# Last layer of a fused four-block kernel: a new order on four engines, rounding inside the scaling, the output shared between ScalarE and GpSimd

## The reference, cut to what matters

```python
def rmsnorm(x): return x * rsqrt(mean(x * x, -1) + EPS)
def act_quant(x):
    scale = 127.0 / clip(max(abs(x), -1), 1e-05)
    return clip(round(x * scale), -128.0, 127.0) / scale
def bitlinear(x, w, b): return act_quant(rmsnorm(x)) @ weight_quant(w).T + b
...
x = x + tanh(g_xattn[1]) * aligned(ctx_1024, layernorm(x))      # 0/1 matrix of the path times ctx
h = gelu(bitlinear(layernorm(x), w1, b1))                       # 256 -> 1024
x = x + tanh(g_ffn[1]) * bitlinear(h, w2, b2)                   # 1024 -> 256
```

## Time and profile before

| | |
|---|---|
| time, 3 runs | 1986.56 us median (1986.07 to 1990.5) |
| the profiled execution | 1983.74 us, its span 1981.8 us |
| start of the last layer | 1628.93 us into the span, so 352.9 us of it |
| busy over the whole span | PE 74%, DVE 73%, ACT 56%, POOL 31% |
| mean granted TensorE clock | 0.877 of full speed |

### The profile page before, as it was taken

One profiled execution on the slowest core, in us unless ns is written; L12 is line 12 of the kernel. 1 busy time (PEld: TensorE's weight loads), 2 busy tenths in 40 slices (PEclk: granted clock), 3 DMA queues, 4 the chain that ended last, 5 costly groups with the idle time before them and its releaser, 6 DMA issues. The chain is left out here.

```text
span 1981.8 us, 35784 instructions
## 1 busy us (share of the span) xinstructions
PE 1476.4 (74%) x10821; PEld 1063.2 (54%) x10821; DVE 1447.5 (73%) x4096; ACT 1101.0 (56%) x2310; POOL 623.9 (31%) x1067
## 2 busy tenths in 40 slices
PE   2689999999999999999999986132331007888886
PEld 1467777777777777777777765000000004555554
DVE  7466666676666667666666643799998988888885
ACT  0166666666666666666666662243333006777876
POOL 3112322222222222322222222200000007888886
PEclk9699999999999999999999998555555559999999
DMA  2444444444443444434444410322210012222210
GB/s 77 122 128 137 120 111 126 110 132 119 125 120 109 129 114 136 118 109 126 111 133 115 113 39 17 89 61 58 60 36 4 0 31 70 81 80 81 81 60 33
DMA packets 322937, 179.49 MB, mean 91 GB/s; under 512 B 93794, under 2 KB 318194, under 8 KB 322803
## 3 DMA queue, kind: packets, MB, share of 16 engines
q1 hardware_dynamic: 322802, 178.07, 32.4%
HBM read 122.91 MB, written 50.33 MB: 87 GB/s over the span
## 5 line engine op out<-in xcount | busy, mean ns | idle before, releaser
L795 DVE TENSOR_REDUCE nmax<-s 128x2 f32<-128x512 f32 x512 | 325.3, 682 | 40.8 <-PE s L376 39.4
L591 ACT ACTIVATE pt<-s 128x512 f32<-128x512 f32 x512 | 277.3, 597 | 84.5 <-PE s L391 84.5
L882 POOL TENSOR_TENSOR r<-rl 128x512 f32<-128x512 f32 x128 | 133.1, 1040 | 371.0 <-ACT rl L621 368.4
L376 PE MATMUL s<-kst,qst 96*128 96x256 bf16 x1024 | 164.1, 276 | 17.7 <-DVE nmax L795 12.7
L391 PE MATMUL s<-qst,kst 128*128 128x256 bf16 x1024 | 167.9, 276 | 9.1 <-ACT pt L591 1.4
L1294 PE MATMUL gate<-diag,one 128*128 128x512 f16 x35 | 21.2, 606 | 176.4 <-DVE left L1381 176.4
L621 ACT ACTIVATE rl<-wb,fscl 128x256 f32<-128x256 f32 x256 | 107.3, 472 | 81.2 <-PE wb L473 81.2
L469 PE MATMUL wb<-x2l,wfcT 128*128 128x256 f32 x512 | 143.2, 301 | 0.5 <-ACT dd L641 0.5
L403 PE MATMUL oacc<-pt,vw 128*32 128x256 f32 x2048 | 137.9, 387 | 2.0 <-ACT pt L591 2.0
L893 POOL TENSOR_TENSOR ln_y<-ln_v,ln_pow 128x6 f32<-128x6 f32 (+2 forms) x37 | 44.5, 1202 | 300.5 <-DVE ln_v L828 300.4
L340 PE MATMUL wb<-wprT,r2l 128*128 128x256 f32 x512 | 129.4, 292 | 6.9 <-DVE r2l L764 6.9
(11 more groups left out here) (265 smaller groups left out, 3998.0 us busy)
## 6 DMA issues: line engine op xcount, KB each, us to landing
kst<-k_parts_dram SPq DMA_DIRECT2D x384, 64.0 KB, 2.7
qst<-q_parts_dram SPq DMA_DIRECT2D x384, 64.0 KB, 2.4
k_parts_dram<-kp SPq DMA_DIRECT2D x32, 384.0 KB, 5.1
q_parts_dram<-qp SPq DMA_DIRECT2D x32, 384.0 KB, 3.1
xin<-in_x_dram SPq DMA_DIRECT2D x32, 256.0 KB, 2.9
cT<-in_ctx_T_dram SPq DMA_DIRECT2D x32, 256.0 KB, 2.7
xres<-in_x_dram SPq DMA_DIRECT2D x32, 256.0 KB, 3.1
cin<-in_ctx_dram SPq DMA_DIRECT2D x32, 256.0 KB, 4.5
```

What stands on the lines that cost most here:

```text
L376: last = pe.matmul(s1[h % 2][:, t, :], qst[b.p][0:MAXROW, h, t * P:t * P + P], kst[b.p][0:MAXROW, h, :], start=True, stop=True)
L591: act.activation(pt[h % (2 * HPG)][:], s2[h % 2][:], ACT.Exp).then_inc(e["expd"], 1)
L795: v.tensor_reduce(nmax[:, T * h:T * h + T], s1[h % 2][:], AX.X, ALU.max, negate=True)\
L882: pool.tensor_tensor(r2[:], rl[:, k % 2], rl[:, k % 2], ALU.mult)\
```

## The change

In the last layer only:

- The constant added by `scale_x` and `scale_h` grows by 26112, so that the low 16 bits of each fp32 word are, read as an f16 number, 1536 plus the rounded value. TensorE transposes these 16 bits of each word (`low16`, every second f16 element of the tile), and the ScalarE copies out of PSUM take 1536 away. `round_x` (ScalarE) and `round_h` (GpSimd) are gone. `xqT_copy` becomes two instructions, since the inverse parts (`xinv`) stay bf16.
- `factors` is divided: GpSimd's `bounds` ends with `back`; VectorE's `factors` has the reciprocal in place of the power of -1, and the product `q`. The hidden part of both belongs to batch k-1 instead of k.
- VectorE's `output` is divided: ScalarE `scale_output` writes po times scale to `yo`, GpSimd `output` adds `x3b`.
- The order on each engine is new; hidden activations are turned and multiplied two turns after their batch's number (k-2) instead of one, the output follows at k-3, and the loop has one turn more. `gl`, `hr`, `x3b` have more buffers. GpSimd's `bias` waits for the masks of a later batch (`masked`), which VectorE now makes in front of gelu's maxima.

```diff
+F16_ONE_AND_A_HALF = 1536.0
+MAGIC_F16 = MAGIC + float(0x6600)
...
-        x3b = [sb(f"x3b{p}", [P, T, D]) for p in range(6)]
+        x3b = [sb(f"x3b{p}", [P, T, D]) for p in range(8)]
...
-        gl = [[sb(f"gl{p}{t}", [P, F]) for t in range(T)] for p in range(2)]
+        gl = [[sb(f"gl{p}{t}", [P, F]) for t in range(T)] for p in range(3)]
-        hr_ = [sb(f"hr{t}", [P, F]) for t in range(T)]
-        hq = [[sb(f"hq{p}{t}", [P, F], BF16) for t in range(T)] for p in range(2)]
+        hr_ = [[sb(f"hr{p}{t}", [P, F]) for t in range(T)] for p in range(2)]
...
-        FIRST, LAST = -6, NB + 2
+        FIRST, LAST = -6, NB + 3
...
+        def low16(words):
+            return words.bitcast(F16).rearrange("p (f two) -> p f two", two=2)[:, :, 0]
...
-                if there(k - 2):
-                    store(k - 2)
+                if there(k - 3):
+                    store(k - 3)
...
             def turn_x(n):
-                w("x_round", n + 1), w("inv_parts", n + 1), w("xqT_cp", n)
-                for c in range(C + 1):
-                    for t in range(T):
-                        last = pe.transpose(pt_x[:, c, t * P:t * P + P], xq[:, t, c * P:c * P + P], identb[:])
+                w("x_scaled", n + 1), w("inv_parts", n + 1), w("xqT_cp", n)
+                for t in range(T):
+                    for c in range(C):
+                        pe.transpose(pt_x[:, c, t * P:t * P + P].bitcast(F16), low16(xr[:, t, c * P:c * P + P]), one16[:])
+                for t in range(T):
+                    last = pe.transpose(pt_x[:, C, t * P:t * P + P], xinv[:, t, :], identb[:])
                 last.then_inc(e["xq_t"], 1)
...
-            def hidden(n):
...
+            def hidden(n, t):
+                w("xqT_cp", n + 1), w("gelu", 2 * (n - 1) + t + 1)
...
             def turn_h(n, t):
-                w("h_round", 2 * n + t + 1), w("hqT_cp", 2 * n + t)
+                w("h_scaled", 2 * n + t + 1), w("hqT_cp", 2 * n + t)
                 for f in range(FT):
-                    last = pe.transpose(pt_h[:, f, :], hq[n % 2][t][:, f * P:f * P + P], identb[:])
+                    last = pe.transpose(pt_h[:, f, :], low16(hr_[n % 2][t][:, f * P:f * P + P]), one16[:])
                 last.then_inc(e["hq_t"], 1)
...
             def output(n):
-                w("x4_res", n)
+                w("o_scaled", n)
...
             for k in range(FIRST, LAST):
+                if there(k - 2):
+                    turn_h(k - 2, 0)
                 if there(k + 1):
-                    hidden(k + 1)
-                if there(k - 1):
-                    turn_h(k - 1, 0)
+                    turn_x(k + 1)
                 if there(k + 4):
                     expand(k + 4)
-                if there(k - 1):
-                    turn_h(k - 1, 1)
-                    output(k - 1)
-                if there(k + 2):
-                    turn_x(k + 2)
+                if there(k - 2):
+                    turn_h(k - 2, 1)
+                if there(k + 1):
+                    hidden(k + 1, 0)
+                    hidden(k + 1, 1)
+                if there(k - 2):
+                    output(k - 2)
...
-            def round_x(n):
-                w("x_scaled", n + 1), w("xq_t", n)
-                act.activation(xq[:, :, 0:D], xr[:], ACT.Copy, bias=-MAGIC).then_inc(e["x_round"], 1)
-
             def xqT_copy(n):
                 w("xq_t", n + 1), w("h_mm", 2 * n)
-                act.activation(xqT[:], pt_x[:], ACT.Copy).then_inc(e["xqT_cp"], 1)
+                act.activation(xqT[:, 0:C, :], pt_x[:, 0:C, :].bitcast(F16), ACT.Copy, bias=-F16_ONE_AND_A_HALF)
+                act.activation(xqT[:, C, :], pt_x[:, C, :], ACT.Copy).then_inc(e["xqT_cp"], 1)
 
             def hqT_copy(n, t):
                 w("hq_t", 2 * n + t + 1), w("o_mm", n)
-                act.activation(hqT[t][:], pt_h[:], ACT.Copy).then_inc(e["hqT_cp"], 1)
+                act.activation(hqT[t][:], pt_h[:], ACT.Copy, bias=-F16_ONE_AND_A_HALF).then_inc(e["hqT_cp"], 1)
+
+            def scale_output(n):
+                w("o_mm", n + 1), w("x4_res", n - 1)
+                for t in range(T):
+                    last = act.activation(yo[n % 2][:, t, :], po[:, t, :], ACT.Copy,
+                                          scale=back[(n + 1) % 4][:, T + t:T + t + 1])
+                last.then_inc(e["o_scaled"], 1)
 
             w("ends", 1)
             for k in range(FIRST, LAST):
+                if there(k - 3):
+                    scale_output(k - 3)
+                if there(k - 2):
+                    hqT_copy(k - 2, 0)
+                if there(k + 1):
+                    xqT_copy(k + 1)
                 if there(k):
+                    squares(k, 0)
                     squares(k, 1)
                 if there(k + 6):
                     distance(k + 6)
-                if there(k - 1):
-                    hqT_copy(k - 1, 0)
+                if there(k - 2):
+                    hqT_copy(k - 2, 1)
                 if there(k + 1):
                     gelu(k + 1, 0)
-                if there(k - 1):
-                    hqT_copy(k - 1, 1)
-                if there(k + 1):
                     gelu(k + 1, 1)
-                if there(k + 2):
-                    round_x(k + 2)
-                if there(k + 1):
-                    squares(k + 1, 0)
-                if there(k + 2):
-                    xqT_copy(k + 2)
...
             def bias(n):
-                w("x3_res", n + 1), w("x4_res", n - 5)
-                for t in range(T):
-                    last = pool.tensor_tensor(x3b[n % 6][:, t, :], x3[:, t, :], b2[:], ALU.add)
+                w("x3_res", n + 1), w("x4_res", n - 7), w("masked", min(n + 3, NB))
+                for t in range(T):
+                    last = pool.tensor_tensor(x3b[n % 8][:, t, :], x3[:, t, :], b2[:], ALU.add)
                 last.then_inc(e["x3_bias"], 1)
 
+            def output(n):
+                w("o_scaled", n + 1)
+                if n >= 2:
+                    pool.wait_ge(o_out[n % 2], 16 * (n // 2))
+                for t in range(T):
+                    last = pool.tensor_tensor(xo[n % 2][:, t, :], yo[n % 2][:, t, :], x3b[n % 8][:, t, :], ALU.add)
+                last.then_inc(e["x4_res"], 1)
...
+                w("xq_t", n), w("factors", n + 1)
...
-            def round_h(n, t):
-                w("h_scaled", 2 * n + t + 1), w("hq_t", 2 * (n - 2) + t + 1)
-                pool.tensor_scalar(hq[n % 2][t][:], hr_[t][:], -MAGIC, 1.0, ALU.add, ALU.mult)\
-                    .then_inc(e["h_round"], 1)
-
-            def factors(nx, nh):
-                p = nh % 2
+            def bounds(k):
+                nx, nh, p = k + 2, k - 1, k % 2
                 c = slice(0 if there(nx) else T, 2 * T if there(nh) else T)
-                yy, aa = y[:, c], tmp[:, c]
...
-                pc.link(pool.tensor_tensor(yy, var[p][:, c], powers[:, 0, c], ALU.pow))
+                pc.link(pool.tensor_tensor(yy, var[p][:, c], powers[:, c], ALU.pow))
                 pc.link(pool.tensor_tensor(aa, amax[p][:, c], yy, ALU.mult))
                 pc.link(pool.tensor_scalar(aa, aa, 1e-5, 1.0 / 127, ALU.max, ALU.mult))
-                pc.tick(pool.tensor_tensor(q0[p][:, c], aa, powers[:, 1, c], ALU.pow))
-                w("gelu", 2 * (nx - 3)), w("x4_res", nh - 3)
-                pc.link(pool.tensor_tensor(back[nh % 4][:, c], aa, ws4[:, c], ALU.mult))
-                w("x_scaled", nx - 1), w("h_scaled", 2 * (nh - 1))
-                pool.tensor_tensor(q[p][:, c], q0[p][:, c], yy, ALU.mult).then_inc(e["factors"], 1)
-
-            pc.tick(pool.memset(xq[:, :, D:D + P], 0.0))
-            pc.tick(pool.memset(powers[:, 0, :], -0.5))
-            pc.tick(pool.memset(powers[:, 1, :], -1.0))
+                w("gelu", 2 * (nx - 3)), w("o_scaled", nh - 3)
+                pool.tensor_tensor(back[k % 4][:, c], aa, ws4[:, c], ALU.mult).then_inc(e["bounded"], 1)
...
             for k in range(FIRST, LAST):
-                if there(k + 2) or there(k):
-                    factors(k + 2, k)
+                if there(k + 2) or there(k - 1):
+                    bounds(k)
+                if there(k + 3):
+                    bias(k + 3)
+                if there(k - 3):
+                    output(k - 3)
                 if there(k + 2):
                     inverse_parts(k + 2)
-                if there(k + 3):
-                    bias(k + 3)
-                if there(k):
-                    round_h(k, 0)
-                    round_h(k, 1)
...
-            def output(n, t):
-                w("x3_bias", n + 1), w("o_mm", n + 1)
-                if n >= 2:
-                    v.wait_ge(o_out[n % 2], 16 * (n // 2))
-                ins = v.scalar_tensor_tensor(xo[n % 2][:, t, :], po[:, t, :], back[n % 4][:, T + t:T + t + 1],
-                                             x3b[n % 6][:, t, :], ALU.mult, ALU.add)
-                if t == T - 1:
-                    ins.then_inc(e["x4_res"], 1)
-
             def scale_x(n):
```

(92 more changed lines are left out.)

34 lines of the change are left out of this document (18 added, 16 removed).

## The result

The changed kernel takes 1933.24 us (median of 4 runs, 1930.39 to 1935.8), the kernel before 1988.39 us in the same comparison: ratio 0.9722, 95% interval 0.97 to 0.9745. The profiled span is 1928.6 us against 1981.8, and the median fell by 55 us where 43 were forecast. 1933.24 lies at the lower edge of the range, inside it by 0.24 us. Medians and ratios here are those of fast executions; one slow one of E9 (3509.33 us) is left out.

The account below looks back on a forecast made before the run. A ScalarE-TensorE ring, with GpSimd's round nearly equal and the low clock added, bounded the kernel at 10.25 us per turn. New span 1646.75 + 31 x 8.6 + 25.7 = 1939, 43 less, so 1944 us; range 1933 to 1965.

Parts of the forecast that it names:

- case A: Last layer: ScalarE, with VectorE close, sets a turn of 8.3 to 8.8 us, 1934 to 1950 us in all; 62%.
- both ends of the pipeline: First hidden group about 1.1 us later, behind an expansion; tail after the last hidden group 3 us longer.
- The two bounds of before: Last layer before: a ScalarE-TensorE ring of 9.81 us per turn at full clock, and GpSimd's round at nearly 9.8.
- The ring of ScalarE and TensorE: Last layer before: the two engines each wait for the other, 9.81 us per turn; the change cuts this ring.
- The low clock: TensorE's half-speed stretches in the last layer cost 0.42 us per turn before; 0.1 was kept after the change.
- ScalarE 8.5, VectorE 8.2: Work per turn in the changed last layer: ScalarE 8.5 us sets the turn, VectorE 8.2 us follows.
- The reciprocal and the product: VectorE's new small instructions for the factors add 0.45 us per turn, waits for their results included.
- The held-back bias: GpSimd's bias waits for VectorE's masks, so both masks take 0.33 us: 0.29 us less per turn.
- B: Rival on TensorE's transposes: strided weight loads are slow, turn 9.2 to 9.4 us, 1962 to 1969 us; 14%.
- E: Rival: strided transposes no faster than one fp32 expansion matmul, 0.22 us each; turn 10.7 us, 2009 us; 5%.
- C: Rival on waits between engines: seven hand-overs of 0.2 us each make a 9.0 us turn, 1956 us; 13%.
- D: Rival: late GpSimd makes a ring through bias, output, inverse parts; turn 9.8 to 10.1 us, 1981 to 1990; 6%.

Follow-up runs that it names:

- E9: The changed kernel run again, unedited, on one chip with the kernel of E4: 1934.77 us, ratio 0.9732 to the kernel before.
- E2: The kernel before with only the rounding part of the change (larger constant, strided transposes, no rounding passes), old order kept: 1957.07 us, ratio 0.9845.
- E1: The kernel before with 18 idle transposes per turn where TensorE waits for the turned x: 1976.28 us against 1987.6.
- E7: The changed kernel with two extra GpSimd passes of 128x1024 on constant data per turn: 1969.67 us, ratio 0.9921 to the kernel before.
- E4: The changed kernel with VectorE's maxima of x in front of the reciprocal and `q`: 1924.55 us, ratio 0.9689 to the kernel before.
- E3: The changed kernel with the output back as one VectorE pass, without ScalarE's scaling and GpSimd's add: 1940.81 us, ratio 0.976 to the kernel before.
- E5: The changed kernel without the wait of GpSimd's bias for the masks: 1964.92 us, ratio 0.99 to the kernel before.

## Why the prediction was right, and where its terms were off

The time fell into the range by 0.24 us, and just below the 1934 to 1950 of case A. What bounded the kernel before and what was taken away was right; which engine comes next was not, and both ends of the pipeline were reckoned too long in sum.

**The two bounds of before.** Right. The ring of ScalarE and TensorE takes 9.36 us when the rounding of x is out of it (E2). GpSimd's round holds the turn at 9.82 with TensorE's gap filled (E1), and at 9.80 when its 2.1 us are put back into the changed kernel (E7).

**The low clock.** Right in size for the kernel before: 12 to 13 us expected of its removal, 11.3 measured (E1). Wrong in what was left: 0.1 us per turn was kept, and there is none.

**ScalarE 8.5, VectorE 8.2: mis-sized, and in the wrong order.** "So ScalarE at 8.5 is next, with 0.3 behind it VectorE" failed. ScalarE needs 8.33 in the changed kernel (8.52 less 0.19 of idle time; 8.22 in E4). VectorE needs 8.52. Two terms of its sum were off. The reciprocal and the product were put at 0.45 with their waits and took 0.84 (1713.31 - 1712.47), because the product waits for GpSimd's second add; E3 and E4 take that away by two different ways and both read 0.16. And the wait behind `residual`, which `xo` had covered, was left out: the next start comes after 0.78 us instead of 0.66. A part of that came back elsewhere (behind `var` the next start comes after 0.07 us instead of 0.19). ScalarE was put too long and VectorE too short; that the larger of the two came out at 8.52, where the sum had 8.5 and 0.1 for the low clock, is luck. The prediction named the question ("whether `xo` meets such an instruction, only the changed trace shows") and then priced it at nothing.

**The held-back bias.** Its sign was right, its price not: 0.29 us was taken from the one slow mask of the earlier trace rows. In the new order the wait for the masks is worth 1.24 us per turn (E5), since without it three VectorE instructions meet three adds, where with it one, `q`, meets one.

The GPSIMD Engine Reference of the Trainium skill (Specifications) names both kinds of VectorE instruction that contend: a 2-port mode, and two SBUF inputs. The runs agree with both: the fp32 `mask`, `var` and `xc` with one SBUF input, and `q` with two, wait; the maxima and the reciprocal, which ran beside adds too, don't. In which mode an instruction runs no view names.

**Strided transposes (B and E).** Taken as nothing, measured as nothing: 0.61 us for eight, as before. The rule of SBUF — State Buffer (Door 1: The DMA port swizzle) in the Trainium skill gave the same.

**Hand-overs and a late GpSimd (C and D).** Neither shows. TensorE waits 0.41 us for `hr`, and as long again in front of the expansion, and ScalarE 0.19 us for the first transposes in each turn; all three are slack behind VectorE. `inverse_parts` begins at 1713.24, after the product's reciprocal is long there, and is in time.

**The turns at both ends: this is where most of the difference lies.** The span came out 10.5 us shorter than the 1939 of the sum. The sum took 31 turns of 8.6, 266.6 us; they took 254.1, which is 12.5 less. The 24 full turns give 1.9 of that. The first four took 26.8 us (1649.45 to 1676.29) instead of 34.4, and the last three 22.7 instead of 25.8. There batches are missing on some engines: in the first two turns, 5.33 and 5.63 us, VectorE has no `hr` yet, and up to 1676 there is no output to add, so `q` takes 0.17 to 0.18. The kernel before has the same at its ends: the earlier trace rows show 16.3 us for its first two turns, not twice 10.25, and this row was not used for the sum.

On the other side the first hidden group comes 5.0 us later in its phase instead of 1.1. Of this 2.7 lie between the transposes of x and the group, where the expansion now stands; it ran at 1.2 GHz (3.72 us for eight matmuls at 1645.93) and was priced at full clock. The other 2.3 lie in front of the transposes, which waited 2.62 us for the inverse parts: these stand behind `bias` on GpSimd, and `bias` behind the masks. The tail was +2.4, forecast +3.

## What to carry to other kernels

When several engines are within some ten per cent of each other, sum each engine's starts, waits for its own results included, not its busy time: VectorE was the bound here at 8.23 busy of 8.52. Ask of every GpSimd instruction which VectorE instruction runs beside it. The count of instructions that meet matters more than their length: `var` of two elements lost 0.53 us, `q` of four 0.33, two masks of 256 together 1.03. Put reductions there (the maxima kept their time), and keep tiny products away from large adds. A pipeline's first and last turns are shorter than the steady one; read them from rows, and price what now stands in front of the first one.

## What the runs showed of the hardware that was not expected

A VectorE instruction of two elements (`var`, 0.16 us alone) took 0.69 us beside an add of GpSimd of 0.84 (E5), and one of four elements (`q`) 0.50; the adds themselves were hardly longer (1.52 for two instead of 1.42). GpSimd's pieces wait as well: in the changed kernel the last `xinv` took 0.54 beside `hr`, against 0.19 for one before it. TensorE's low clock went away in E1 by added work and in E2 without any, with 1.6 us of idle time before each hidden group left; what decides it stays open.
